# First layer of a two-layer attention and expert kernel: mask rows inside two-head score operands, four small routing steps fewer on VectorE, the projected result in another PSUM bank

## The reference, cut to what matters

```python
def _L0_xattn_ref(q, k, v, attention_mask, Wq, bq, Wk, bk, Wv, bv, Wo, bo):
    qm = _split_heads(q @ Wq.T + bq)
    km = _split_heads(k @ Wk.T + bk)
    vm = _split_heads(v @ Wv.T + bv)
    scores = jnp.einsum('bnlh,bnph->bnlp', qm, km) / np.sqrt(HEAD_DIM)
    scores = jnp.where(attention_mask[:, None, None, :], scores, -1e8)
    attn = jax.nn.softmax(scores, axis=-1)
    out = jnp.einsum('bnlp,bnph->bnlh', attn, vm)
    return out.transpose(0, 2, 1, 3).reshape(B, L, D_MODEL) @ Wo.T + bo

def _L0_ffn_ref(x, w_gate, w1, w2):
    topk_vals, topk_idx = jax.lax.top_k(xt @ w_gate, 2)
    gates = jax.nn.softmax(topk_vals, axis=-1)
    out = sum(gate_e * (relu(xt @ w1[e]) @ w2[e]) for the two chosen experts e)

x = x + _L0_xattn_ref(_layernorm(x), ctx_1024, ctx_1024, mask, ...)
x = x + _L0_ffn_ref(_layernorm(x), L0_ffn_w_gate, L0_ffn_w1, L0_ffn_w2)
```

## Time and profile before

| what | us |
|---|---|
| median of 3 runs | 924.11 (921.0 to 926.9) |
| the profiled execution | 923.89 |
| its span, first to last instruction | 921.6 |
| TensorE busy in the span | 879.5 (95%) |
| ScalarE busy | 690.0 (75%) |
| VectorE busy | 669.9 (73%) |
| GpSimd busy | 447.0 (48%) |
| mean granted TensorE clock | 0.987 of full |

### The profile page before, as it was taken

One profiled execution on the slowest core, in us unless ns is written; L12 is line 12 of the kernel. 1 busy time (PEld: TensorE's weight loads), 2 busy tenths in 40 slices (PEclk: granted clock), 3 DMA queues, 4 the chain that ended last, 5 costly groups with the idle time before them and its releaser, 6 DMA issues.

```text
span 921.6 us, 29215 instructions
## 1 busy us (share of the span) xinstructions
PE 879.5 (95%) x8399; PEld 785.6 (85%) x8399; DVE 669.9 (73%) x2146; ACT 690.0 (75%) x2694; POOL 447.0 (48%) x739
## 2 busy tenths in 40 slices
PE   5899999999999879999997999999999999999996
PEld 3677777778777769999996899999999999999995
DVE  6799999999999742222216888887877877877773
ACT  2999998999989623333347999997887788788782
POOL 4135443544444541111126777776666666666542
PEclk9999999999999979999999999999999999999998
DMA  5877677767776222222220222222121121122110
GB/s 164 254 219 231 210 229 234 230 213 240 227 234 213 67 81 68 69 72 71 69 89 21 62 64 65 67 69 56 52 65 60 46 68 60 43 68 63 34 52 10
DMA packets 113565, 103.93 MB, mean 113 GB/s; under 512 B 11762, under 2 KB 100628, under 8 KB 113495
## 3 DMA queue, kind: packets, MB, share of 16 engines
q1 hardware_dynamic: 106594, 88.81, 30.9%
q0 software_dynamic: 6112, 13.90, 4.9%
q10 hardware_dynamic: 788, 0.39, 0.1%
HBM read 56.53 MB, written 46.53 MB: 112 GB/s over the span
## 4 chain that ended last, share of the span: by engine, by line
PE 87%; DVE 3%; issue 3%; SPq 3%; ACT 2%; DMA 2%; POOL 0%; DVEq 0%; ACTq 0%; POOLq 0%
PE bank L1160 11%; PE bank L1394 10%; PE bank L1409 7%; PE bank L1366 7%; PE bank L1373 7%; PE bank L1419 6%; PE bank L1207 6%; PE bank L1480 6%; PE bank L1468 4%; PE bank L1491 3%; PE bank L1200 3%; PE bank L1197 3%; PE bank L1182 2%; PE bank L1318 2%; PE bank L1278 2%
## 5 line engine op out<-in xcount | busy, mean ns | idle before, releaser
L675 ACT ACTIVATE PR<-PR,nmx 128x128 f32<-128x128 f32 x512 | 198.1, 391 | 3.8 <-DVE nmx L879 0.5
L675 ACT ACTIVATE PR<-bank,nmx 128x128 f32<-128x128 f32 x512 | 185.7, 415 | 1.0 <-DVE nmx L879 1.0
L345 POOL TENSOR_TENSOR PR<-PR,rden 128x512 f32<-128x512 f32 x128 | 133.5, 1043 | 98.9 <-DVE rden L884 98.9
L1160 PE MATMUL bank<-ident,PR 128*128 128x128 f32 x1024 | 154.7, 276 | 1.8 <-DVE YT L890 1.0
L1160 PEld LDWEIGHTS bank<-ident,PR 128*128 128x128 f32 x1024 | 120.5, 142 | 41.9 <-issue 34.8
L675 ACT ACTIVATION_READ_ACCUMULATOR PR<-bank,nmx 128x1 f32 x512 | 131.1, 256 | 0.0
L769 ACT ACTIVATE H<-bank 128x512 f32<-128x512 f32 x70 | 41.8, 597 | 93.2 <-PE bank L1366 93.2
L1394 PE MATMUL bank<-XCT,wqk 128*128 128x128 f32 x832 | 103.7, 278 | 0.7 <-ACT XCT L663 0.7
L1394 PEld LDWEIGHTS bank<-XCT,wqk 128*128 128x128 f32 x832 | 96.9, 192 | 3.5 <-ACT XCT L663 1.0
L675 ACT ACTIVATION_READ_ACCUMULATOR PR<-PR,nmx 128x1 f32 x512 | 97.1, 190 | 0.0
L879 DVE TENSOR_REDUCE nmx<-bank 128x4 f32<-128x512 f32 x128 | 87.7, 686 | 9.3 <-PE bank L1200 7.3
(11 more groups left out here) (196 smaller groups left out, 2093.4 us busy)
## 6 DMA issues: line engine op xcount, KB each, us to landing
second_layer_values<-wide SPq DMA_DIRECT2D x32, 512.0 KB, 3.6
wide<-second_layer_values SPq DMA_DIRECT2D x32, 512.0 KB, 3.3
expert_outputs<-HF SPq DMA_DIRECT2D x32, 256.0 KB
expert_outputs<-HF SPq DMA_DIRECT2D x64, 128.0 KB, 2.1
KBD<-expert_outputs SPq DMA_DIRECT2D x128, 64.0 KB
QS<-expert_outputs SPq DMA_DIRECT2D x32, 256.0 KB
PR<-expert_inputs SPq DMA_DIRECT2D x36, 128.0 KB, 2.0
expert_outputs<-PR POOLq DMA_DIRECT2D x35, 128.0 KB, 2.0
```

What stands on the lines that cost most here:

```text
L345: nc.gpsimd.tensor_tensor(unit, unit, rden[:, p, G * g:G * g + G].unsqueeze(2).broadcast_to([P, G, P]), ALU.mult).then_inc(s["nm"], 1)
L675: last = nc.scalar.activation(PR[:, g, j * P:(j + 1) * P], scored, ACT.Exp, bias=nmx[:, p, h:h + 1], accum_out=den[:, p, h:h + 1])
L1160: last = nc.tensor.transpose(T_BANK[g % 2][:, j * P:(j + 1) * P], PR[:, g, j * P:(j + 1) * P], ident[:])
```

## The change

Four things in the first part. Scores: `QS` and `KBD` hold eight pairs of heads instead of four units of four. A pair has 64 rows (4 x 2 x 8) and three more: ones in `QS`, and the mask rows of its sequence in `KBD`. A unit is two products of 256 columns over 67 rows. The mask rows of all sequences are made once, as 96 rows, stored to DRAM, and loaded with the keys of each sequence (two loads of keys, one of mask rows, on a semaphore for each parity); the bf16 rows and their products are gone. Expert choice: MAX8 and the index search read the scores in PSUM and write the tables of all sequences; the sums of the slot numbers are written straight as scatter rows, and GpSimd copies them to `slot_f` behind the scatters. The projected result goes to columns 256 to 383 of bank 7 (`R_BANK`), and the waits of both banks' users change with it. The order on TensorE: the routing transpose stands ahead of unit 1's transposes, the counts stand behind the scores of unit 1.

```diff
+PAIR_ROWS = 4 * 2 * DH0
+ROWS = PAIR_ROWS + 3
+KEY_LOADS = 3
...
+        mk_dram = nc.dram_tensor("key_mask_rows", (NB, 3, P), FP32, kind="Internal").ap()
...
+        R_BANK = bank[7][:, 2 * P:3 * P]
...
-            KBD = first_layer.enter_context(nc.sbuf_tensor("KBD", [P, 2, NU, G, P], FP32R))
-            QS = first_layer.enter_context(nc.sbuf_tensor("QS", [P, 2, NU, P], FP32R))
-        KEYS = sb("KEYS", [P, KEYS_A, PAIRS, P])
+            KBD = first_layer.enter_context(nc.sbuf_tensor("KBD", [P, 2, PAIRS, 2, P], FP32R))
+            QS = first_layer.enter_context(nc.sbuf_tensor("QS", [P, 2, PAIRS, P], FP32R))
+        KEYS = sb("KEYS", [P, KEYS_A + 1, PAIRS, P])
...
-                    sp.dma_start(mk3[0:3, :], flat_mask.partition_broadcast(3)).then_inc(ld_mask, 16)
+                    sp.dma_start(mk3[0:3 * NB, 0:P], mask_keys.unsqueeze(0).broadcast_to([3, NB, P])).then_inc(ld_mask, 16)
...
+                if n == -2:
+                    sp.wait_ge(mk_made, 1)
+                    sp.dma_start(mk_dram.rearrange("m r s -> r m s"), mk_rows[0:3 * NB, :]).then_inc(mk_stored, 16)
...
+                    if is_sequence(0, n + 1):
+                        sp.wait_ge(mk_stored, 16)
                     wait_apart(sp, (a["kw"], 16 * (n + 2)), (a["s"], NU * (n)))
-                    for j in range(G):
-                        rows = spread(q, 1).rearrange("(g j x) s -> j x g s", g=NU, j=G)[j]
-                        sp.dma_start(KBD[32 * j:32 * j + 32, q, :, j, :].bitcast(FP32), rows).then_inc(a["bd"], 16)
+                    for j in range(2):
+                        rows = spread(q, 1).rearrange("(k j x) s -> j x k s", k=PAIRS, j=2)[j]
+                        sp.dma_start(KBD[32 * j:32 * j + 32, q, :, j, :].bitcast(FP32), rows).then_inc(a[f"bd{q}"], 16)
+                    sp.dma_start(KBD[PAIR_ROWS:ROWS, q, :, :, :].rearrange("r k j s -> r (k j) s").bitcast(FP32),
+                                 mk_dram[n + 1].unsqueeze(1).broadcast_to([3, NH, P])).then_inc(a[f"bd{q}"], 16)
                     wait_apart(sp, (a["qw"], 32 * (n + 2)), (a["s"], NU * (n)))
-                    sp.dma_start(QS[:, q, :, :].bitcast(FP32),
-                                 spread(q, 0).rearrange("(g x) s -> x g s", g=NU)).then_inc(a["qs"], 16)
+                    sp.dma_start(QS[0:PAIR_ROWS, q, :, :].bitcast(FP32),
+                                 spread(q, 0).rearrange("(k x) s -> x k s", k=PAIRS)).then_inc(a["qs"], 16)
...
+                    nc.gpsimd.tensor_copy(slot_f[:, :, bass.ds(m, 1)], scat_idx[:, p, :].unsqueeze(2)).then_inc(rt["slots"], 1)
...
+            nc.vector.memset(QS[PAIR_ROWS:ROWS, 0, :, :].bitcast(FP32), 1.0)
...
+                    nc.vector.memset(QS[PAIR_ROWS:ROWS, 1, :, :].bitcast(FP32), 1.0)
+                    for r in range(3):
+                        link(nc.vector.memset(mk_part[r * NB:(r + 1) * NB, :], bf16_parts(FILL0)[r]))
                     dve.wait_ge(ld_bqk, 32)
                     dve.wait_ge(ld_mask, 32)
                     link(nc.vector.tensor_scalar(bqk[:, 0:1], bqk[:, 0:1], float(DH0) ** -0.5, None, ALU.mult))
+                    nc.vector.tensor_scalar(mk_rows[0:3 * NB, :], mk3[0:3 * NB, 0:P], -1.0, mk_part[0:3 * NB, 0:1],
+                                            ALU.add, ALU.mult).then_inc(mk_made, 1)
...
-                    link(nc.vector.tensor_copy(pcol[:], bank[2][:, 2 * P:2 * P + 1]))
-                    dve.wait_ge(rows_zeroed, 2)
-                    nc.vector.tensor_scalar(mk_rows[0:3, 0:4 * P], mk3[0:3, 0:4 * P], -1.0, pcol[0:3, 0:1],
-                                            ALU.add, ALU.mult).then_inc(set_copy, 1)
+                    nc.vector.tensor_copy(wo0T[:], bank[2][:, P:2 * P]).then_inc(set_copy, 1)
                     link(nc.vector.memset(VZ[:, 1], 0.0))
-                if n == 1:
-                    nc.vector.tensor_scalar(mk_rows[0:3, 4 * P:16 * P], mk3[0:3, 4 * P:16 * P], -1.0, pcol[0:3, 0:1],
-                                            ALU.add, ALU.mult)
                 if n == 2:
-                    nc.vector.tensor_scalar(mk_rows[0:3, 16 * P:], mk3[0:3, 16 * P:], -1.0, pcol[0:3, 0:1],
-                                            ALU.add, ALU.mult).then_inc(set_copy, 1)
                     dve.wait_ge(ld_mk, 32)
-                    dve.wait_ge(rows_zeroed, 4)
+                    dve.wait_ge(rows_zeroed, 3)
...
-                    nc.vector.tensor_reduce(slot_f[:, :, bass.ds(n - 4, 1)].rearrange("p k o -> p (k o)"), picked[:], AXX,
-                                            ALU.add).then_inc(rt["slots"], 1)
+                    if exists(n - 6):
+                        wait(dve, rt[f"sc{p}"], 2 * loads(n - 6, p))
+                        wait(dve, rt["slots"], n - 5)
+                    with nc.allow_low_precision(reason="sums of one row number and zeros"):
+                        nc.vector.tensor_reduce(scat_idx[:, p, :], picked[:], AXX, ALU.add).then_inc(rt["placed"], 1)
                 if exists(n - 3):
                     dve.wait_ge(rt["lg"], n - 2)
-                    nc.vector.tensor_copy(lgs[:], M_BANK[:, 0:NE]).then_inc(rt["lgc"], 1)
-                    wait_apart(dve, (rt["lgc"], n - 2))
-                    nc.vector.max(top8[:], lgs[:]).then_inc(rt["top8"], 1)
-                if exists(n - 4):
-                    wait_apart(dve, (rt["slots"], n - 3), (rt[f"sc{p}"], 2 * loads(n - 6, p) if exists(n - 6) else 0))
-                    nc.vector.tensor_copy(scat_idx[:, p, :].unsqueeze(2), slot_f[:, :, bass.ds(n - 4, 1)]).then_inc(rt["placed"], 1)
+                    nc.vector.max(top_v[:, n - 3, :], M_BANK[:, 0:NE]).then_inc(rt["top8"], 1)
...
-                    nc.vector.max_index(topi[:], top8[:], lgs[:]).then_inc(rt["topi"], 1)
-                    nc.vector.tensor_copy(topv[:, :, bass.ds(n - 3, 1)], top8[:, 0:2].unsqueeze(2))
+                    nc.vector.max_index(top_e[:, n - 3, :], top_v[:, n - 3, :], M_BANK[:, 0:NE]).then_inc(rt["lgc"], 1)
                 if exists(n - 2):
                     norm_alone_apply(dve, rt, n - 2)
                 if exists(n - 3):
-                    wait_apart(dve, (rt["topi"], n - 2))
-                    nc.vector.tensor_copy(tope[:, :, bass.ds(n - 3, 1)], topi[:, 0:2].unsqueeze(2)).then_inc(rt["tope"], 1)
-                    wait(dve, rt["tope"], n - 2)
+                    wait(dve, rt["lgc"], n - 2)
                     nc.vector.tensor_tensor(hot1[:], iota_e[:].unsqueeze(1).broadcast_to([P, 2, NE]),
-                                            tope[:, :, bass.ds(n - 3, 1)].broadcast_to([P, 2, NE]), ALU.is_equal).then_inc(rt["hot"], 1)
+                                            top_e[:, n - 3, 0:2].unsqueeze(2).broadcast_to([P, 2, NE]),
+                                            ALU.is_equal).then_inc(rt["hot"], 1)
...
-                    mm(S_BANK[g % 2][:].rearrange("p (j k) -> p j k", j=G), ones3[:],
-                       mk_rows[:, bass.ds(m * P, P)].unsqueeze(1).broadcast_to([P, G, P]), start=True, stop=False,
-                       skip_group_check=True)
-                    mm(S_BANK[g % 2][:], QS[:, p, g, :], KBD[:, p, g, :, :].rearrange("p j s -> p (j s)"),
-                       start=False, stop=True, skip_group_check=True).then_inc(a["s"], 1)
+                    for k in range(2):
+                        last = mm(S_BANK[g % 2][:, 2 * k * P:2 * (k + 1) * P], QS[0:ROWS, p, 2 * g + k, :],
+                                  KBD[0:ROWS, p, 2 * g + k, :, :].rearrange("r j s -> r (j s)"), start=True, stop=True)
+                    last.then_inc(a["s"], 1)
...
-                    transpose_unit(a, n - 1, 1)
                 if exists(n - 3):
                     pe.wait_ge(rt["xn"], n - 2)
                     wait(pe, rt["lgc"], upto(n - 4))
@@ -1228,15 +1219,18 @@
                         wait(pe, rt["xct"], upto(n - 4))
                     nc.tensor.transpose(M_BANK[:, 0:P], XND[:], ident[:]).then_inc(rt["tr"], 1)
                 if exists(n - 1):
+                    transpose_unit(a, n - 1, 1)
...
-                    wait(pe, a["rts"], upto(n - 2))
-                    if isinstance(n, int):
-                        wait(pe, a["xct"], upto(n + 1))
+                    wait(pe, rt["xct"], upto(n - 3))
+                    if isinstance(n, int):
+                        wait(pe, rt["lgc"], upto(n - 4))
+                        wait(pe, rt["next"], upto(n - 5))
                         wait(pe, a["x"], upto(n - 3))
-                    mm(M2_BANK[:, 0:P], OT0[:, p, :], wo0T[:], start=True, stop=False)
-                    mm(M2_BANK[:, 0:P], ones3[:], brow[:, 1, :], start=False, stop=True).then_inc(a["o"], 1)
+                    mm(R_BANK, OT0[:, p, :], wo0T[:], start=True, stop=False)
+                    mm(R_BANK, ones3[:], brow[:, 1, :], start=False, stop=True).then_inc(a["o"], 1)
...
+                if is_sequence(NB + 1, n):
+                    project_keys(0, 0)
+                    project_keys(0, 1)
+                if exists(n + 2):
```

(22 more changed lines are left out.)

62 lines of the change are left out of this document (24 added, 38 removed).

## The result

The change makes the kernel no faster. After takes 928.73 us (median of 20 runs, 926.1 to 931.33), before 926.41 (20 runs, 920.1 to 929.6): ratio 1.0029, 95% interval 1.0015 to 1.0042. The forecast was 912. The profiled execution of before (span 921.6) was one of its quicker ones; that of after has a span of 926.3, and the two traces differ by 4.7 us.

A forecast was written before the change was run, and what follows sets the result against it. The first layer was taken as TensorE-bound, with ScalarE's work next. From 923.9: less 1.6 (start), less 15.7 (29 steps), plus 1.0 (loads in the last four loop steps), plus 4.5 (drain) = 912.1, predicted 912.0 us; range 905 to 923.

The forecast's parts named there:

- The regular step: First layer, 29 steps: mean falls from 9.13 to 8.59 us, stalls included, 15.7 us gained.
- TensorE then needs 8.08 us: TensorE's work in a layer step: 9.00 less 0.92 us; at the other end 8.72.
- the term of the mask products: Score units on TensorE: mask products go, new products take 0.11 us a pass, saving 0.92 us a step (0.28 at least).
- ScalarE, which is not changed, is late next: ScalarE in a layer step: 0.48 us is waiting, its work of 8.34 us sets the new step.
- The loop through three engines: Layer step, chain from unit 3's scores through TensorE, VectorE and ScalarE back to them: 8.55 us falls to 8.1.
- the projection's new wait: Projection on TensorE in a layer step: also waits for VectorE's copy of the routing's transposed rows, 0.1 us where it bites.
- Rival (b): Layer steps: new products cost their weight loads, or the copy wait ties VectorE and TensorE; step 8.90, 920 us, chance 0.22.
- Rival (e): Layer steps: no shorter step, since ScalarE's wait keeps its place for another reason; 927 us, chance 0.04.
- The two stalls stay: TensorE's two query-load stalls in the layer, the longer 1.44 us: unchanged, held within the 0.13 us a step.
- Rival (d): Layer steps: TensorE waits for late operand loads in every step, on fewer partitions plus a third load; 948 us, chance 0.07.
- The start: Up to the exponentials of sequence 2: two load issues less and no mask-row work, 1.6 us gained, between 0.5 and 3.
- The drain: End of the first layer: VectorE waits for GpSimd's slot-number copies before the totals, 4.5 us lost (3.1 to 4.9).

The follow-up runs named there:

- e9: On e6, ScalarE's first copy of the wide values cut from 512 columns to 64 in the loop steps: 917.0 us, 0.9886 of before.
- e10: On e6, ScalarE's second copy of the wide values cut from 512 columns to 64 in the loop steps: 917.5 us, 0.9880 of before.
- e7: On e1, the projected result put back in bank 5, with the old waits: 925.4 us, 1.0003 of before.
- e3: Kernel before without mask products, each score product cut into two of 256 columns: 921.4 us, 0.9942 of before.
- e6: On e1, large loads moved behind the query load or spread over loop pieces 1 to 4: 918.5 us, 0.9935 of before.
- e4: Kernel after without the third key load, that of three mask rows: 927.4 us, 1.0019 of before.
- e2_no_mask_product: Kernel before without the four mask products of a step, nothing in their place: 920.4 us, 0.9946 of before.
- e1: Kernel after with VectorE writing the slot numbers and casting them into scatter rows again, GpSimd's copy gone: 924.0 us, 0.9987 of before.

## Why the prediction was wrong

- **The regular step** is the step that failed, and 29 x 0.54 = 15.7 us with it. The 8.59 us of the forecast held 0.13 for stalls and loop ends; 9.14 came. Without them it was 8.46, and 8.91 came.
  - "TensorE then needs 8.08 us": the term of the mask products was mis-sized, 0.92 us where the products of a step went from 9.00 us to 8.75, so 0.25. The slot of 0.11 a pass was taken from L1287, which follows products as long as itself. The pair measured 0.32 on average, between my two ends (0.22 and 0.38) and nearer the upper one, and its neighbours grew. To this comes the pause at the loop's turn, 0.17 us a step on average, which before does not have.
  - "ScalarE, which is not changed, is late next": wrong, e9 and e10 show it. Its 8.34 us was also misread: two steps of different length take turns, and I set one of them (8.82 us; the next is 9.29) beside a mean of 9.00.
  - The loop through three engines left GpSimd out. VectorE did lose its 0.56 us, but 0.18 to 0.25 of it became a wait for GpSimd's copy of the kept rows and 0.28 a wait for the projection. I had named the projection's new wait, 0.1 us; e7 finds nothing for the bank. Of GpSimd I had asked only what it does in the drain.
  - Rival (b) has the first half of its reason right; e3 shows that the cut itself is free, and that what counts is what stood ahead of the product. Its step of 8.90 us looks like the 8.91 measured, but it holds the stalls, and 9.14 is the number beside it. Rival (e), 927 us with a step that doesn't get shorter, is nearest in time by luck: ScalarE did not hold the step, and the regular step did get shorter.
- **The stalls.** "The two stalls stay": wrong. All waits for the query load took 5.5 us more; behind sequence 2, the two long steps took 3.4 us more. Rival (d) had the right wait and the wrong cause and place: not in every step, and neither the 64 partitions (e3, e6) nor the third load (e4) make the most of it. A shorter step does not help a transfer that stands behind bulk; e2_no_mask_product, with the loads of before, lost part of its gain at the same place too (a step of 11.5 us, 6.8 us of query waits). Why the stall grew so much more than the step shrank is not shown.
- **The start.** 1.6 us gained was forecast, 3.2 lost: the wait of 4.08 us at sequence 1, and a lower clock. I had counted two issues less, and not what was in the DMA engines ahead of them. But part of the 3.2 is the trace of before, which has a clock of 1.00 there: e2_no_mask_product and e3_no_mask_split, with the same loads as before and less work, start the exponentials of sequence 2 1.1 and 1.2 us later than it, at 0.84 and 0.69 between 20 and 30 us.
- **The drain.** 4.5 us lost was forecast; 4.7 came in the trace, 3.5 of it from the copy by e1's. Mechanism and size right.
- **The clock.** Nothing was forecast for the keys' projection, and nothing came: 16 records took 4.02 us, where before has two pieces of 8 with 2.07 us each (the earlier trace rows has the first). Behind them before's trace lost time at the lower clock that after's did not, the -3.6 us of the result; no term of the sum had it.
- **The base.** The forecast went from 923.9, and the kernel before turned out at 926.4 over 20 runs. 2.5 us of the miss are that.
- The Trainium skill's rule (TensorE: Matmul & The Clock Gate, LDWEIGHTS), by which a weight load of 128 columns takes 0.107 us and the pair so 0.22, an estimate, agrees with the turned units here (L1154: 0.87 us for 8), and not with the score pair: 0.32. From the Trainium skill's rule on ports (SBUF — State Buffer, Door 1: The DMA port swizzle) came an estimate of 0.2 us a step; no regular step of after shows a wait for a load.

## What to carry to other kernels

Price a removed instruction by what is left when it is gone, also by what it covered, and not by its slot: 0.92 us of slots were worth 0.17, and a pause at the loop's turn came to light. When several engines are within some per cent of one another, follow one period of each of them through to its own start, the engine that is half idle too, since a latency through it (here GpSimd's norms and copy) can hold the step as well as work does. Look at what is queued ahead of a load that already stalls before making the loop around it faster: moving bulk loads behind it gave 5 us, where the whole change gave none. And read the granted clock of every stage before comparing two single traces: here 3.6 us went with it in code that the change leaves alone.
